# One order per engine over a whole eight-batch program, in place of four tables of orders by period

## The reference

```
x = L0_attn_x
xn = _layernorm(x, axis=-1)
x = x + _L0_attn_ref(xn, ...) + _L0_ffn_ref(xn, ...)
xn = _layernorm(x, axis=-1)
x = x + _L1_attn_ref(xn, ...) + _L1_ffn_ref(xn, ...)
return x
```

## Time and profile before

| | |
|---|---|
| time, median of 3 runs | 1972.19 us (1971.9 to 1973.89) |
| span of the profiled execution | 1973.4 us |
| PE busy, share of the span | 1742.6 us, 88% |
| DVE busy | 1308.3 us, 66% |
| ACT busy | 980.4 us, 50% |
| POOL busy | 824.0 us, 42% |
| mean granted TensorE clock | 0.945 of full |

### The profile page before, as it was taken

How to read it: one execution, slowest core, us unless ns; L and a number is a source line. 1 busy time by engine, 2 the same in 40 slices (tenths; PEclk the granted TensorE clock), 3 DMA queues, 4 the chain that set the end, 5 groups by cost and what they waited for, 6 DMA issues and landing times.

```text
span 1973.4 us, 44292 instructions
## 1 busy us (share of the span) xinstructions
PE 1742.6 (88%) x16808; PEld 1140.5 (58%) x16808; DVE 1308.3 (66%) x3522; ACT 980.4 (50%) x2545; POOL 824.0 (42%) x827
## 2 busy tenths in 40 slices
...
DMA packets 126627, 90.00 MB, mean 46 GB/s; under 512 B 42168, under 2 KB 113976, under 8 KB 126136
## 3 DMA queue, kind: packets, MB, share of 16 engines
...
...
## 4 chain that ended last, share of the span: by engine, by line
PE 62%; DVE 18%; issue 7%; POOL 6%; ACT 5%; DMA 0%; SPq 0%; DVEq 0%; POOLq 0%; ACTq 0%
PE bank L695 9%; PE bank L1090 3%; PE bank L802 3%; PE bank L725 3%; PE bank L812 3%; PE bank L1076 3%; DVE blk L1579 2%; PE bank L782 2%; PE bank L1048 2%; PE bank L836 2%; PE bank L731 2%; PE bank L1187 2%; PE bank L1167 2%; DVE nmx L1654 2%; PE bank L1075 2%
## 5 line engine op out<-in xcount | busy, mean ns | idle before, releaser
L1371 ACT ACTIVATE shared<-bank 128x512 f32<-128x512 f32 (+1 forms) x384 | 201.8, 531 | 221.9 <-PE bank L1076 219.8
L1846 POOL TENSOR_TENSOR soft<-soft,prec 128x512 f32<-128x512 f32 x128 | 132.8, 1043 | 429.4 <-DVE prec L1489 428.8
L1654 DVE TENSOR_REDUCE nmx<-bank 128x1 f32<-128x512 f32 (+3 forms) x352 | 222.9, 638 | 90.8 <-PE bank L1048 89.8
L1267 ACT ACTIVATE soft<-bank,nmax 128x128 f32<-128x128 f32 x512 | 179.7, 379 | 110.6 <-DVE nmax L1481 109.8
L1807 POOL TENSOR_TENSOR qk_rs<-qk_rs,minus_half 128x16 f32<-128x16 f32 x64 | 188.0, 2937 | 5.3
L725 PE MATMUL bank<-w_sb,hT 128*128 128x512 f32 x256 | 137.7, 626 | 8.8 <-DVE rot L1471 5.7
L1076 PE MATMUL bank<-shared 75*128 75x384 bf16 (+3 forms) x512 | 144.7, 311 | 0.0
L1075 PE MATMUL bank<-b_sb 128*128 128x128 bf16 x512 | 115.7, 227 | 25.6 <-ACT shared L1371 24.9
L1048 PE MATMUL bank<-shared 72*128 72x256 bf16 (+3 forms) x512 | 127.3, 301 | 0.0
L695 PE MATMUL bank<-c_sb,soft 128*128 128x128 f32 x608 | 101.6, 297 | 15.9 <-POOL soft L1846 8.1
L1090 PE MATMUL bank<-shared,vaug 128*32 128x512 f32 (+3 forms) x1024 | 99.0, 486 | 18.5 <-ACT shared L1371 13.7
...
## 6 DMA issues: line engine op xcount, KB each, us to landing
...
vm<-v_f SPq DMA_DIRECT2D x112, 128.0 KB, 2.4
parts_dram<-parts SPq DMA_DIRECT2D x96, 128.0 KB, 2.4
...
```

The costliest lines, as they stand in the source:

```text
L1267: a = af(v4(p_sb, 2, 4)[:, j, g], place("fS", j)[:, g * P:(g + 1) * P], ACT.Exp, bias=nmax[:, at:at + 1], accum_out=psums[:, at:at + 1])
L1371: af(v4(PTm, 2, GROUP)[:, u % 2, i, 0:n], place("mST", b, i)[:, 0:n], ACT.Exp).then_inc(mexp_done, 1)
L1654: reduce(v3(nmx[:], HM)[:, h:h + len(heads), c], v3(place("mS", b, t)[:, 0:len(heads) * (c + 1) * P], len(heads)), AX, ALU.max, negate=Tru ...
L1846: tt(p, p, spread(prec[:, at:at + NPAIR], P), ALU.mult).then_inc(fnorm_done, 1)
```

## The change

The four strings per engine are replaced by one string over all periods, and `walk` no longer stops at the end of a period: the streams of all periods are joined, and a letter takes the next step of its stream, whichever period that step belongs to. The steps, their instructions, waits and increments are the same, and so is the order inside each stream. Of 2464 steps on PE 1261 stand at another place, on average by 1.1 places; on ACT 885 of 1512, on DVE 820 of 1640, on POOL 196 of 536, on SP 144 of 216.

```
-        (
-         "fedefdefdeeffdffedeeeeffebeffebbfbfbfbfffbbfdbddbdddfdbdddbbdbdbddddffddbddddbdbdddbdbddbedddbdbbbbbbdbddddddd"
+     "fedefefefddedffedefeeeffebefebfbbbfffbfffbbfdbdddbddfddbfddddbbfddbdddbdbdddddbdbdddbddbdbddddbdbbbbdbbddbdddeddd"
...
-def period(p):
-
-    if p == 0 or p == LAST:
-        one, two = (part(q) for q in ((-1, 0) if p == 0 else (LAST, BATCH)))
-        return {s: one[s] + two[s] for s in STREAMS}
-    return part(p)
+def streams():
+
+    parts = [part(p) for p in range(-1, BATCH + 1)]
+    return {s: [x for one in parts for x in one[s]] for s in STREAMS}
...
 def walk(engine, parts):
 
-
-
-    for p in range(BATCH):
-        left = {s: collections.deque(x for x in steps if x[0] in parts) for s, steps in period(p).items()}
-        for s in ORDER[engine][0 if p == 0 else p - BATCH + 4 if p >= BATCH - 2 else 1]:
-            if left[s]:
-                name, *at = left[s].popleft()
-                parts[name](*at)
-        assert not any(left.values()), (engine, p, {s: list(x)[:2] for s, x in left.items()})
+    left = {s: collections.deque(x for x in steps if x[0] in parts) for s, steps in streams().items()}
+    for s in ORDER[engine]:
+        name, *at = left[s].popleft()
+        parts[name](*at)
+    assert not any(left.values()), (engine, {s: list(x)[:2] for s, x in left.items()})
```

More of the change, by code:

```diff
@@ L86 @@
[L86 to L103 removed]
+     "fedefefefddedffedefeeeffebefebfbbbfffbfffbbfbdddbddfddbfddddfbbddbdddbdbdddddbdbdddbddbdbddddbdbbbbdbbddbdddeddd"
@@ new lines @@
+     "amaammaamamaaaccaaccaacccaaccmaacccaccaacaacacacaccaacccaccaacccaccacaacccaaccaacccaccaccccccccccccccccccccccccc"),
+    "ACT": (
+     "fefefefedfddfeeddeefefffbfbbfbfffffbbbbdfdfdfbbbfdbdfddddddbdbddbdddddddbbbbddddeffdddffffffbdebbfefbeefffdffbbe"
+     "bedefebffebfbbbfffbbbbffbbdddfffddfffbbfbbmbfmffbfdddbbbdmffdddmmmfdmdfdbffdddbbdbdddmbdbbddbdbddmddbedbmffffdfm"
+     "fffbcffcbbccbmcccfcffccbfccbcbmcbcfccefccecffcebcecbbcebffccfcbcececfbbefcbeccbcccffcccffcbcccfcfcccfccfcccbddcb"
+     "dbbddddbmfmffbbffbbddmmmmddddddfmdffdbdddbbfdbfddddddmbbbbdbddmddedbbmfffffmfffdbcffmcbcbcbfccccffccbfcmccbbcfcb"
+     "ccefccefcfecbfcebcbcbcffeccbcefcecebbcfbeccbcccffcccfbfccccffcccfccfccccbcdbddddbbddmbmffffbbbbddddmffdddmmdmdmf"
+     "fdbddfdbbddbfmdbdbbbddddbddmdddbebmffffffdmffbcffcbcbcbmccfcfcfccbfccfbbcmcbcccecfcefcfcebcecbfbfcebccfcbcefcecf"
+     "bbcebcecbcfcccffcccfbcccccfccccccfcfbcdbdfbbdddbmdmdddfffbfdbbddbfmmmddfmmddffdbfdddbbddbfmdddbbbdbddbddmdddbebm"
+     "fdfffffmffbcfcbbcmcfbccfccffccbfccmfcbbcbcfcceccefcfcebcecbbcbcfffeccbcececbbffcebcecbcccffcccffcbccccccccccccfd"
+     "cfddbbffdbbdbmdmdffddffdbbbbfmmmmfdddddffmddbdbddbfdbfmbbbddddbdddbddmdddbebmffdffffmffbcffcbcbcmfbccccffccbfcfc"
+     "bbcmccbccecfeffccecbcecfbbfcbecfccbcefcecefbbcebccbcfcccfccffbcccfccfcccccfcccbdcbdddbbfdmdbmfdfffbbfbbdmddddddm"
+     "mfmddmffdbdfbddbdddbmfbdddbbbddbddmdeddbbmfffffmfffdbfcfmcbbccfbccccffccbfccmcbbfcfcbccececfcfecbcefbcbcbecffccb"
+     "cececfebbfcbeccbcfccfcccffcbcccccfccffcccccdddcddbfddddbbbmmffbfddffdddddbddddbbdfbmmffdddmbmbbmddddbffddbddbdbm"
+     "bbmbmdbffcccffcfccffmcffccbfccbcbcbmffffccfbccmbcbcbfccfcfcccbcbfbfcbcccbccbbcbcbccccccbcccccccbccccccmmmmmmmmmm"
+     "mmmccccccccccccccccccccccccccccccccccccccccccccccccccccc"),
```

99 lines of the change are left out of this document (43 added, 56 removed).

## The result

The changed kernel takes **1914.9 us** (median of 4 runs, 1907.0 to 1920.54) against 1973.04 us (4 runs, 1971.9 to 1974.17): a ratio of 0.9701, 95% interval 0.9675 to 0.9728. Measured once more at the end of the study it took 1907.57 us (5 runs) against 1972.56, ratio 0.9679 (0.9658 to 0.9699). On three chips some runs of the kernel before took 1992 to 1996 us at a granted clock of 0.933 to 0.935 (2 of 25 beside `e5`, `e6`, `e7` and `e9`, 6 of 19 beside `e8` and `e10` to `e12`, 7 of 19 beside `e13` and `e14`), and the ratios taken there count them, so the medians stand beside such a ratio; a run of 6867 us of `e1` and one of 4152 us of before beside it are in no ratio.

What follows compares the result with a forecast made beforehand. PE was taken as the bound, idle in holes at the period ends. From 1973.4 us, 7.2 (end of period 0), 17.1 (ends of periods 1 to 6) and 2.0 (the end) came off: 1947.1, stated as 1946 us, range 1924 to 1967.

Steps and rivals of the forecast that it cites:

- Bound and place: PE bounds the full stretches; its idle holes at the period ends are where moved work wins time.
- End of period 0: Four qT, bg, inv_v and an fqk of batch 1 move into PE's idle time there: 7.2 us, between 0 and 15.0.
- Fills at the ends of periods 1 to 5: Two fqk and two qT fill PE's waits at mST, matg and aT: 3.0 us per end, 2.1 at period 4.
- `solve` ahead of `x1` on DVE I also count at nothing: DVE, period ends: solve moved before x1 gains nothing; xn2T(1) on PE only must not wait.
- rival C: Solve before x1 makes PE wait at xn2T at five ends once the 2.4 us margin is gone: 1984 us, chance 0.06.
- The sum above takes this as unchanged: PE's granted clock, 0.50 from 496 to 508 us, stays as it was; no gain counted.
- Rival A: Clock stays up at the six period ends, 6 x 4.2 = 25 us more: 1921 us, chance 0.15.
- Inside period 0: PE moves there fell under all other moves, in stretches where PE is full: counted at nothing.
- End of period 6: Filled waits of PE, priced like the other period ends: 3.0 us.
- Tail: DVE, 1880 to 1928 us: one eu, one ew and one e_down leave the row maxima, 2.0 us, between 0 and 2.5.
- Rival B: Filled time at the period ends is given back as waits elsewhere, a chain setting the period: 1963 us, chance 0.15.

Runs made afterwards that it cites:

- e5: Kernel before with solve moved ahead of x1 on DVE at the ends of periods 1 to 6: 1974.02 us, ratio 1.0.
- e6: Changed kernel with solve put back right behind x1 on DVE at the ends of periods 1, 3, 4, 5, 6: 1950.31 us, ratio 0.9897.
- e7: Kernel before with two fqk moved around an mST and two qT around matg on PE, ends of periods 1 to 5: 1974.17 us, ratio 1.0001.
- e9: Kernel before with two extra fqk matmuls, their result overwritten, on PE at the ends of periods 1 to 5: 1992.93 us, ratio 1.0059.
- e8: Changed kernel with the fqk and qT fills undone at the ends of periods 1 to 5, solve left in front: 1933.93 us, ratio 0.976.
- e10: Kernel before with the edits of e5 and e7 together: 1972.97 us, ratio 0.9959.
- e12: Changed kernel with solve ahead of x1 at the end of period 2 too: 1914.26 us, ratio 0.9657.
- e13: e10 with the cover of the softmax put back as in the new order, ends of periods 1 to 5: 1977.53 us, ratio 0.9961.
- e14: e13 with solve back behind x1 on DVE at the ends of periods 1 to 6: 1984.09 us, ratio 1.0002.
- e1: Kernel before with the new order only up to PE step 127, inside period 0: 1967.79 us, ratio 0.9969.

## Why the prediction was wrong, point by point

- *Bound and place.* Right: the holes at the period ends held the time, and nothing moved on DVE, ACT or POOL (busy times within 3 us of before).
- *End of period 0*, 7.2 us: the mechanism held. The 4.70 us before `xn2T(0)` is now 0.96, the stretch is 8.4 us shorter, 12.0 us when it is done alone. The size was near in the profile (6.5 us of idle time) and low against the run alone.
- *Fills at the ends of periods 1 to 5*, 4 x 3.0 + 2.1 = 14.1 us (the parts of the 2.1, 0.72 + 0.87 + 0.69, add up to 2.3): the size is close to what stands in the ledger (13.2 us of idle time) and to what taking them out costs (12 to 20 us). The reason given was wrong: "I take what the filled waits themselves measure, because 98% of the following 90 us are PE's". `e7_fill_only` filled the same waits and won nothing, since 2.61 us opened at `fPT`.
- **The step of the mechanism that failed: "`solve` ahead of `x1` on DVE I also count at nothing".** It was costed as a risk (rival C) and never as a condition. The new order can put `xn2T` ahead of `qT` and `fS` ahead of `final`, and so keep the softmax covered, only because `x1_apply` comes early; put back, it costs 35 us, twice the 17.1 us of the whole term for the period ends, 17.7 of it at the ends of periods 1 to 5 and 12.9 at the end of period 6. Rival C did not come, but by less than its margin of 2.4 us: at the end of period 1 `solve` to `x1_apply` took the 14.7 us that it was priced at, and PE met `xn2T(1)` 0.1 us after `x1_apply` ended: it came 14.8 us after the last `fa`, where 17.1 were reckoned, at a clock of 1.00 where 0.50 had stood. That the Gram step comes first was needed: with it put back `xn2T(1)` waits 3.02 us. At the ends of periods 4 and 6, which rival C counted too, `solve` did wait for its input, and a later `xn2T` took it up.
- **The step that failed by most in the number: "The sum above takes this as unchanged"**, of the clock. The profiled span is 28.3 us below the sum (1947.1 - 1918.8); 21.9 of them are PE work that no longer runs at the lower clock, and 6.4 are idle time (32.7 for 26.3). Rival A had this as the forecast less 25 us, at a chance of 0.15, and the range ended 3 us above its price. Where waits were filled, less time ran at the lower clock (`e9_idle_fill` shows it with no work moved), so a forecast that fills waits cannot leave the clock as it was. That rival A's 1921 us and the 1920.54 of the profiled execution agree is in part luck: A put its 25 us at the six period ends, which gave 15.4, and the rest came from period 0 and from idle time.
- *Inside period 0*, counted at nothing: 6.0 us alone, 9.2 in the profile, of which 7.7 is PE work, 5 to 6 of it the clock (0.90 to 0.93).
- *End of period 6*, 3.0: 11.8 us in the profile, mis-sized by far. The 2.31 us of `aT` behind `solve` there was not in my rows, only the five ends like it were read. With `solve` put back behind `x1` (`e6`) it is 12.9 us longer. What else it holds was not taken apart.
- *Tail*, 2.0: 3.8 us of idle time, as forecast in kind but larger, and 3.1 us given back at the lower clock in this execution.
- *Rival B* (given back elsewhere) fell for the whole change and was right for the fills alone: `e7` has the new wait at `fPT` that it named.
